# Ranks and slots one and two turns sooner, and one exponential for all shares, in the routing stage of a two-layer graph network

## The chip, the core and the metric

The kernel runs on one core of one Trainium2 chip. The metric is the device time of one execution in microseconds, the median of the runs. Five engines work side by side, each through its own row of instructions: TensorE (PE in the profile), VectorE (DVE), ScalarE (ACT), GpSimd (POOL) and SyncE (SP). They meet at semaphores.

## What is computed

Two layers, each a graph part, a mixer and a mixture of experts, on 3125 nodes with 256 numbers each. The change lies where layer 1 goes from the graph part to its experts. Cut to that, the reference reads:

```python
agg = segment_sum((xn @ weight)[src] * edge_weight[:, None], dst)      # second graph part
x = x + relu(agg) + mixer(xn)
tokens = layernorm(x)                                                   # no scale, no shift
probs = softmax(tokens @ router_w.T)
rw, re = top_k(probs, 2)                                                # two experts of eight
rw = rw / rw.sum(-1)
x = x + tokens + sum over e of combine[:, e] * (gelu(tokens @ w1[e] + b1[e]) @ w2[e] + b2[e])
```

The two shares of a token are the softmax of its two largest logits: with a = exp(second - first) they are 1 / (1 + a) and 1 minus that.

## The kernel before

The program is a row of stages; each ends with a barrier of all engines. The stage of interest is `second_graph`. The 3125 nodes are 25 tiles of 128 (`T`, g = 0 to 24). The sums over edges are already in `agg`. The stage multiplies them by the weight, adds them to `x`, normalizes, finds each token's logits and its two experts, gives each (token, expert) pair a row of the table `slots_d` in DRAM, expert after expert, and scatters the tokens there. The next stage, `second_experts`, reads that table in tiles of 128 rows, and multiplies each by its expert's weights.

Work goes through a software pipeline written out by hand: `pipeline(engine, [(lag, step), ...])` lets the engine run turn after turn, and in turn n each step takes tile n - lag, in the order of the list. Here it is all written out, with no loop left in the program (`first=NI, last=NI`). Turn by turn:

- TensorE: `turn_sums` (L2383, transposes), `project` (L2391, the weight), `turn_n` (L2400, transposes of normalized tokens), `score` (L2408, the logits), `rank_picks` (L2422, L2423).
- VectorE: `residual` (L2228, L2231, L2233: sum, statistics), `invert` (L2238, L2240), `place_picks` (L2284 to L2291) and `route` (L2254 to L2272).
- ScalarE: copies of TensorE's results (L2337, L2357, L2365), `spread_of` (L2344, a square root), `norm_x` (L2350), `exp_apart` (L2372, an exponential).
- GpSimd: two indirect DMAs a tile (L2211), 50 in all, each scatters 128 rows of 260 numbers.

The choice of experts works on groups of tiles, called parties: `PARTY = [3, 4, 4, 4, 4, 3, 3]`. For a party, `route` takes the logits in `pr`, finds the largest, its expert, and the second with its expert, and counts each expert's tokens tile by tile in `so_far`. `rank_picks` finds with two matmuls how many tokens ahead of this one chose the same expert. `place_picks` makes row numbers of these ranks (`slot`), and signals `slots_ready`, for which GpSimd waits. A step for parties does something only in the turn of the party's last tile. Before the change the lags are: `route` 6, `rank_picks` 8, `exp_apart` 8, `place_picks` 9. So for party 0, whose last tile is 2, VectorE chooses in turn 8, TensorE ranks in turn 10, and VectorE places in turn 11. `link(...)` makes VectorE wait for its own last instruction.

After the pipeline VectorE has a tail: the two shares from the exponentials (L2308 to L2310), then the number of tiles of each expert, and for each of 56 slot tiles its expert and its first row (`tile_expert`, `tile_at`, L2312 to L2329), which the next stage reads.

Of the kernel before, what the change touches and what calls it, by code (L numbers as in the profile page):

```python
# [6 lines left out]
ALU = mybir.AluOpType  # L7
ACT = mybir.ActivationFunctionType
# [12 lines left out]
R = 5  # L21
# [44 lines left out]
PARTY = [3, 4, 4, 4, 4, 3, 3]  # L66
PARTY_END = [sum(PARTY[:n + 1]) for n in range(len(PARTY))]
# [2086 lines left out]
def second_graph(nc, A, hold, bank, const, acc, agg, share, tile_expert, tile_at, bias1, bias2, slots_d, emptied, big_v, w, w_r, xrow):  # L2154
# [5 lines left out]
    with Stage(nc) as ctx:  # L2160
# [6 lines left out]
        most, place = S.sb("most", [P, 3, G]), S.sb("place", [P, 2, G])  # L2167
# [5 lines left out]
        r_step, apart, apart_exp, set_up = (S.sem(n) for n in ("r_step", "apart", "apart_exp", "set_up"))  # L2173
# [8 lines left out]
        whole = dict(turns=NI, width=R, first=NI, last=NI)  # L2182
# [8 lines left out]
        def ends_at(g):  # L2191
            return PARTY_END.index(g + 1) if g + 1 in PARTY_END else None
# [26 lines left out]
        def _(dve):  # L2219
            link = Steps(dve, r_step)  # L2220
# [22 lines left out]
            def route(i, j):  # L2243
                k = ends_at(i * R + j)
                if k is None:
                    return
                size = PARTY[k]
                order = const[:, C_ORDER:C_ORDER + E].unsqueeze(1).broadcast_to([P, size, E])
                dve.wait_ge(pr_ready, PARTY_END[k])
                if k > 0:  # L2250
                    dve.wait_ge(apart_exp, k)
                for n in range(2):
                    at = pr[:, k % 2, n, 0:size, :]
                    link(dve.tensor_reduce(most[:, n, 0:size], at, AX, ALU.max))  # L2254
                    link(dve.tensor_tensor(pick[:, n, 0:size], at, wide(most[:, n, 0:size], size), ALU.is_equal))

                    link(dve.tensor_tensor(rank[:, 0:size, :], pick[:, n, 0:size], order, ALU.mult))
                    link(dve.tensor_reduce(most[:, 2, 0:size], rank[:, 0:size, :], AX, ALU.max))
                    link(dve.tensor_tensor(pick[:, n, 0:size], rank[:, 0:size, :], wide(most[:, 2, 0:size], size), ALU.is_equal))
                    if n == 0:  # L2260
                        link(dve.tensor_scalar(xrow[:, PARTY_END[k] - size:PARTY_END[k], D + 1:D + 2],
                                               most[:, 2, 0:size].unsqueeze(2), -1.0, float(E), ALU.mult, ALU.add))
                        link(dve.scalar_tensor_tensor(out=pr[:, k % 2, 1, 0:size, :], in0=pick[:, 0, 0:size], scalar=-BIG, in1=at,
                                                      op0=ALU.mult, op1=ALU.add))
                dve.tensor_tensor(most[:, 2, 0:size], most[:, 1, 0:size], most[:, 0, 0:size], ALU.subtract).then_inc(apart, 1)
                if k > 0:
                    link(dve.tensor_copy(so_far[:, 0, :], so_far[:, PARTY[k - 1], :]))
                link(dve.tensor_tensor(taken[:, 0:size, :], pick[:, 0, 0:size], pick[:, 1, 0:size], ALU.add))
                if k == len(PARTY) - 1:
                    link(dve.tensor_tensor(taken[:, size - 1, :], taken[:, size - 1, :], used[:, :, 0], ALU.mult))  # L2270
                for t in range(size):
                    last = dve.tensor_tensor(so_far[:, t + 1, :], so_far[:, t, :], taken[:, t, :], ALU.add)  # L2272
                    if t < size - 1:
                        link(last)
                last.then_inc(picked, 1)
# [25 lines left out]
                                   ALU.is_ge, ALU.mult))  # L2301
            dve.tensor_copy(xrow[:, :, D:XW], token[:, :].unsqueeze(2).broadcast_to([P, T, XW - D])).then_inc(set_up, 1)
            dve.wait_ge(set_up, 1)
            pipeline(dve, [(1, residual), (2, invert), (9, place_picks), (6, route)], **whole)

            dve.wait_ge(apart_exp, len(PARTY))
            link(dve.tensor_scalar(share[:, 1, :], share[:, 1, :], 1.0, None, ALU.add))  # L2308
            link(dve.reciprocal(share[:, 0, :], share[:, 1, :]))
            link(dve.tensor_scalar(share[:, 1, :], share[:, 0, :], -1.0, 1.0, ALU.mult, ALU.add))  # L2310
            dve.wait_ge(ranked, len(PARTY))
            link(dve.tensor_scalar(tiles[:, :], n_of, 1.0 / P, None, ALU.mult))  # L2312
            link(dve.tensor_tensor(used[:, :, :], tiles[:, :].unsqueeze(2).broadcast_to([P, E, T]),
# [13 lines left out]
                                          in1=first_row[:, :], op0=ALU.mult, op1=ALU.add))  # L2327
            link(dve.tensor_copy(tile_at[:, 0, :], tile_expert[0:1, :]))
            link(dve.tensor_copy(tile_at[:, 1, :], first_row[0:1, :]))  # L2329

        @block.scalar
        def _(act):
# [31 lines left out]
                    once(act, slots_ready, k - 1)  # L2364
                act.activation(pr[:, k % 2, 0, t, :], l_ps, ACT.Copy).then_inc(pr_ready, 1)  # L2365

            def exp_apart(i, j):
                k = ends_at(i * R + j)
                if k is None:
                    return  # L2370
                act.wait_ge(apart, k + 1)
                act.activation(share[:, 1, PARTY_END[k] - PARTY[k]:PARTY_END[k]], most[:, 2, 0:PARTY[k]], ACT.Exp)\  # L2372
                   .then_inc(apart_exp, 1)

            pipeline(act, [(0, copy_sums), (2, spread_of), (3, norm_x), (4, copy_n), (5, copy_logits), (8, exp_apart)], **whole)

        @block.tensor
        def _(pe):
# [44 lines left out]
                pe.matmul(to, ones, so_far[:, 0:size, :].rearrange("p t e -> p (t e)"), start=False, stop=True)\  # L2423
                  .then_inc(ranked, 1)

            pipeline(pe, [(0, turn_sums), (1, project), (4, turn_n), (5, score), (8, rank_picks)], **whole)

def expert_weights(big_v):
# [263 lines left out]
```

## Time and profile before

| | |
|---|---|
| median of 3 runs | 2205.79 us (2203.96 to 2211.8) |
| the profiled execution, its own time | 2211.77 us |
| its span, first to last instruction | 2210.1 us |
| what lies around the span | 1.7 us |
| mean granted clock of TensorE | 0.814 |
| PE, DVE, ACT, POOL busy in the span | 72%, 57%, 40%, 48% |
| this stage in the span | some 1944 to 2051 us |

Times in the trace count from the span's start. A row of the timeline reads: start, duration, engine, line, operation, tiles written and read; in brackets the idle time of the engine before it, and what ended that.
### The profile page before, as it was taken

The page shows a single profiled execution, that of the slowest core. Times are in us where ns is not written, and L with a number is a line of the kernel's source. Part 1 is how long each engine was busy: PE and PEld are TensorE (multiplying, and loading weights), DVE is VectorE, ACT ScalarE, POOL GpSimd, SP SyncE. Part 2 cuts the span into 40 slices and gives each one's busy share as a digit, 9 for nine tenths or more (in the row PEclk, how much of TensorE's full clock was granted, in tenths as well). Part 3 has the DMA queues.
Part 4 walks back from the last instruction along what each step waited for, and adds up shares of the span by engine and source line. Part 5 has one row for each costly group of instructions (what it writes and reads, how often), then busy time and mean ns, then how long its engine had stood idle before and what let it go on. Part 6 is the DMA issues. An engine that isn't in the chain of part 4 may idle for free. (4 is left out here: it accounts for less than half of the span.)

```text
span 2210.1 us, 31483 instructions
## 1 busy us (share of the span) xinstructions
PE 1599.5 (72%) x7770; PEld 1248.9 (57%) x7770; DVE 1250.0 (57%) x3879; ACT 874.0 (40%) x2979; POOL 1068.4 (48%) x1173
## 2 busy tenths in 40 slices
PE   5535677666766676969999766776787776974792
PEld 4533444444444445959999654555565555763792
DVE  3523655556556587855777634554555554675435
ACT  2221655665656586645777421000011000153451
POOL 2751666666666500421222256666666666225341
PEclk8665677777777797989999777888888888995896
DMA  5741544444444302836555232333333333122786
GB/s 188 218 141 38 152 121 123 125 133 123 129 128 126 98 18 73 264 109 203 181 165 179 73 99 84 89 91 90 88 90 89 88 91 93 42 87 80 219 263 222
DMA packets 176882, 276.92 MB, mean 125 GB/s; under 512 B 28920, under 2 KB 132218, under 8 KB 176456
## 3 DMA queue, kind: packets, MB, share of 16 engines
q0 software_dynamic: 50352, 136.58, 21.5%
q1 hardware_dynamic: 82194, 94.23, 14.0%
q10 hardware_dynamic: 44166, 44.14, 6.0%
q8 instruction: 71, 1.16, 0.2%
q14 instruction: 99, 0.81, 0.1%
HBM read 202.35 MB, written 73.58 MB: 125 GB/s over the span
## 5 line engine op out<-in xcount | busy, mean ns | idle before, releaser
L501 POOL DMA_INDIRECT ring<-feat_d,src_lane x440 | 433.0, 984 | 282.9 <-issue 121.5
L1221 POOL DMA_INDIRECT rows<-xn_d,src_of x416 | 404.2, 972 | 236.3 <-issue 106.0
L1201 PE MATMUL bank<-ring,a_hot 128*128 128x260 f32 x880 | 319.0, 511 | 147.9 <-DVE ring L1100 64.7
L1392 PE MATMUL bank<-rows,big 128*128 x880 | 288.9, 445 | 138.8 <-DVE big L1300 66.7
L1130 ACT ACTIVATE ring<-ring 128x64 f32<-128x64 f32 x1540 | 376.7, 336 | 15.8 <-issue 14.8
L1201 PEld LDWEIGHTS bank<-ring,a_hot 128*128 128x128 f32 x880 | 204.8, 251 | 226.0 <-DVE ring L1100 83.6
L1309 DVE TENSOR_TENSOR big<-bank,big 128x256 f32 x440 | 186.6, 424 | 233.4 <-DMA m_bo<-in_L_mix_bo 112.1
L1392 PEld LDWEIGHTS bank<-rows,big 128*128 128x128 f32 x880 | 165.6, 211 | 236.7 <-issue 222.1
L1085 DVE TENSOR_TENSOR acc<-bank,acc 128x260 f32 x440 | 186.8, 425 | 145.9 <-PE bank L1201 59.4
L1362 ACT ACTIVATE big<-bank,a_col 128x256 f32<-128x256 f32 (+1 forms) x26 | 13.1, 553 | 417.4 <-issue 257.2
L1300 DVE TENSOR_SCALAR big<-const,dst_lane,ew_lane 128x128 f32<-128x128 f32 x440 | 151.8, 346 | 1.0 <-PEq L95 1.0
L184 POOL TENSOR_TENSOR e_norm_rstd<-e_norm_mv,const 128x1 f32<-128x1 f32 x75 | 42.7, 570 | 202.4 <-DVE e_norm_mv L180 202.4
L1992 PE MATMUL bank<-xn1T,top_w 128*128 128x128 f32 x800 | 99.6, 280 | 5.5 <-PEq L95 5.5
L1419 PE MATMUL bank<-big 128*128 128x256 f32 (+1 forms) x416 | 96.9, 376 | 5.4 <-ACT big L1372 5.4
L1372 ACT ACTIVATE big<-bank,a_b 128x256 f32<-128x256 f32 (+1 forms) x104 | 42.0, 464 | 145.4 <-PE bank L1419 123.2
L1992 PEld LDWEIGHTS bank<-xn1T,top_w 128*128 128x128 f32 x800 | 96.0, 197 | 5.8 <-issue 5.6
L2211 POOL DMA_INDIRECT slots_d<-xrow,g_slot x50 | 49.4, 987 | 95.9 <-DVE g_slot L2291 82.5
L2004 PE MATMUL bank<-top_w,e_mid 128*128 128x256 f32 x400 | 95.2, 383 | 0.0
L1431 PE MATMUL bank<-big 128*128 128x256 f32 x400 | 94.5, 379 | 0.0
L2499 POOL DMA_INDIRECT y_d<-e_y,e_to x56 | 55.2, 985 | 68.1 <-DVE e_to L2582 65.4
L1419 PEld LDWEIGHTS bank<-big 128*128 128x128 f32 x416 | 77.8, 193 | 18.0 <-issue 7.7
L1431 PEld LDWEIGHTS bank<-big 128*128 128x128 f32 x400 | 76.0, 190 | 10.3
(405 smaller groups left out, 2901.4 us busy)
## 6 DMA issues: line engine op xcount, KB each, us to landing
slots_d<-fold ACTq DMA_DIRECT2D x25, 1300.0 KB, 5.6
e_w_now<-in_L_ffn_w SPq DMA_DIRECT2D x56, 256.0 KB
a_dst_bc<-dst_lo_d SPq DMA_DIRECT2D x23, 512.0 KB
big<-in_L_ffn_W SPq DMA_DIRECT2D x16, 512.0 KB
e_x<-slots_d SPq DMA_DIRECT2D x56, 130.0 KB
ring<-feat_d,src_lane POOLq DMA_INDIRECT x440
rows<-xn_d,src_of POOLq DMA_INDIRECT x416
e_ys<-y_d SPq DMA_DIRECT2D x24, 256.0 KB
```

The costliest lines, as they stand in the source:

```text
L501: pool.indirect_dma_start(ring[:, q % RING, at, :], None, table, bass.IndirectOffsetOnAxis(ap=src_lane[:, n:n + 1], axis=0)).then_inc(gath ...
L1085: dve.tensor_tensor(to, bank[n % BANKS][:, 0:D + H], to, ALU.add).then_inc(added, 1)
L1130: last = act.activation(part[:, 0:DH], part[:, 0:DH], ACT.Copy, scale=part[:, DH:DW])
L1201: pe.matmul(bank[n % BANKS][:, 0:D + H], hot[:, q % HOTS, at, :], ring[:, q % RING, at, :], start=True, stop=True)\
L1221: pool.indirect_dma_start(rows[:, n % RING1, :], None, table, bass.IndirectOffsetOnAxis(ap=src_of[:, n:n + 1], axis=0)).then_inc(gathered[ ...
L1300: dve.tensor_scalar(hot[:, n % HOTS, :], const[:, C_IOTA:C_IOTA + P], dst_lane[:, n:n + 1], edge_weight[:, n:n + 1], ALU.is_equal, ALU.mul ...
L1309: dve.tensor_tensor(to, bank[n % 4][:, 0:D], to, ALU.add).then_inc(added, 1)
L1392: pe.matmul(bank[n % 4][:, 0:D], hot[:, n % HOTS, :], tile_of(rows, slots[n % 4]), start=True, stop=True)\
L1419: last = pe.matmul(mid_ps[q % 2][:, f * 2 * P:f * 2 * P + m * P], w1[:, k, n * P:(n + 1) * P], lnT[:, k, 0:m * P], start=(k == 0), stop=(k ...
L1431: last = pe.matmul(y_ps[:, t * D:(t + 1) * D], mid[:, f, t * P:(t + 1) * P], w2[:, f, :], start=(f == 0), stop=(f == FT - 1))
L1992: last = pe.matmul(mid_ps[half][:, f * P:(f + 1) * P], w1[:, half, k, f * P:(f + 1) * P], xn1T[:, k, bass.ds(g * P, P)], start=(k == 0), s ...
L2004: last = pe.matmul(y_ps[:, 0:D], mid[:, j, n * P:(n + 1) * P], w2[:, half, f, :], start=(n == 0), stop=(n == FT - 1))
```

## The change

Three things change in `second_graph`, and nothing elsewhere.

- `route` writes the difference of the two logits into `share[:, 0, ...]`, a row that is kept for all tiles, where it wrote into the scratch `most[:, 2, ...]`. It no longer waits for the exponential of the party before, but waits for its own subtraction. ScalarE's step `exp_apart`, seven exponentials in the pipeline, becomes one exponential of all 25 tiles behind the pipeline.
- `rank_picks` goes from lag 8 to lag 7 and stands behind `project`, ahead of `turn_n` and `score`; `place_picks` goes from lag 9 to lag 7.
- VectorE's turn begins with `place_picks` and `route`, and ends with `residual` and `invert`. The three instructions that finish the shares go from the head of VectorE's tail to its end.

```diff
@@ route, VectorE
                 dve.wait_ge(pr_ready, PARTY_END[k])
-                if k > 0:
-                    dve.wait_ge(apart_exp, k)
...
-                dve.tensor_tensor(most[:, 2, 0:size], most[:, 1, 0:size], most[:, 0, 0:size], ALU.subtract).then_inc(apart, 1)
+                dve.tensor_tensor(share[:, 0, PARTY_END[k] - size:PARTY_END[k]], most[:, 1, 0:size], most[:, 0, 0:size], ALU.subtract)\
+                   .then_inc(apart, 1)
+                dve.wait_ge(apart, k + 1)
@@ VectorE, pipeline and tail
-            pipeline(dve, [(1, residual), (2, invert), (9, place_picks), (6, route)], **whole)
-
-
-            dve.wait_ge(apart_exp, len(PARTY))
-            link(dve.tensor_scalar(share[:, 1, :], share[:, 1, :], 1.0, None, ALU.add))
-            link(dve.reciprocal(share[:, 0, :], share[:, 1, :]))
-            link(dve.tensor_scalar(share[:, 1, :], share[:, 0, :], -1.0, 1.0, ALU.mult, ALU.add))
+            pipeline(dve, [(7, place_picks), (6, route), (1, residual), (2, invert)], **whole)
+
+
             dve.wait_ge(ranked, len(PARTY))
...
             link(dve.tensor_copy(tile_at[:, 1, :], first_row[0:1, :]))
+            dve.wait_ge(apart_exp, 1)
+            link(dve.tensor_scalar(share[:, 1, :], share[:, 1, :], 1.0, None, ALU.add))
+            link(dve.reciprocal(share[:, 0, :], share[:, 1, :]))
+            link(dve.tensor_scalar(share[:, 1, :], share[:, 0, :], -1.0, 1.0, ALU.mult, ALU.add))
@@ ScalarE
-            def exp_apart(i, j):
-                k = ends_at(i * R + j)
-                if k is None:
-                    return
-                act.wait_ge(apart, k + 1)
-                act.activation(share[:, 1, PARTY_END[k] - PARTY[k]:PARTY_END[k]], most[:, 2, 0:PARTY[k]], ACT.Exp)\
-                   .then_inc(apart_exp, 1)
-
-            pipeline(act, [(0, copy_sums), (2, spread_of), (3, norm_x), (4, copy_n), (5, copy_logits), (8, exp_apart)], **whole)
+            pipeline(act, [(0, copy_sums), (2, spread_of), (3, norm_x), (4, copy_n), (5, copy_logits)], **whole)
+            act.wait_ge(apart, len(PARTY))
+            act.activation(share[:, 1, :], share[:, 0, :], ACT.Exp).then_inc(apart_exp, 1)
@@ TensorE
-            pipeline(pe, [(0, turn_sums), (1, project), (4, turn_n), (5, score), (8, rank_picks)], **whole)
+            pipeline(pe, [(0, turn_sums), (1, project), (7, rank_picks), (4, turn_n), (5, score)], **whole)
```

How the instructions move. VectorE's row, end of the choice of party 0 (one piece of the difference; a line with + is the changed kernel's, and its numbers from L2252 on are two less than before up to L2263):

```order
-L2272 TENSOR_TENSOR g_so_far<-g_so_far,g_taken 128x8 x3
+L2284 TENSOR_TENSOR g_rank<-bank,g_first_slot 128x24
+L2287 TENSOR_TENSOR g_pick<-g_pick,g_rank 128x24 x2
+L2288 TENSOR_REDUCE g_place<-g_pick 128x2x3
+L2291 CAST g_slot<-g_place 128x2x3
 L2228 SCALAR_TENSOR_TENSOR acc<-bank,acc 128x256
 L2231 BN_STATS g_stats<-acc 128x6
```

Before, the choice ends here, at the tail of turn 8; now the slots of party 0 are made here, at the head of turn 9, and its choice stands one residual and one inversion ahead.

TensorE's row, ranks of party 0, before:

```order
L2383 MATMUL bank<-const,big 128x128 x2
L2391 MATMUL bank<-big,g_sumsT 128x256 x2
L2400 MATMUL bank<-const,xrow 128x128 x2
L2408 MATMUL bank<-big,g_nT 128x8 x2
L2422 MATMUL bank<-g_taken,g_before_me 128x24
L2423 MATMUL bank<-g_so_far,const 128x24
```

and of the change (six lines less in their numbers):

```order
L2377 MATMUL bank<-const,big 128x128 x2
L2385 MATMUL bank<-big,g_sumsT 128x256 x2
L2416 MATMUL bank<-g_taken,g_before_me 128x24
L2417 MATMUL bank<-g_so_far,const 128x24
L2394 MATMUL bank<-const,xrow 128x128 x2
L2402 MATMUL bank<-big,g_nT 128x8 x2
```

The ranks stood at the end of turn 10; now they stand within turn 9, with the transposes and the logits of that turn behind them.

ScalarE's row behind party 0, before:

```order
L2365 ACTIVATE g_pr<-bank 128x8
L2372 ACT_TABLE_LOAD
L2372 ACTIVATE share<-g_most 128x3
L2337 ACTIVATE g_sumsT<-bank 128x256
L2344 ACT_TABLE_LOAD
L2344 ACTIVATE g_std<-g_mv,g_eps 128x1
```

and the end of its row in the changed kernel:

```order
L2357 ACTIVATE g_nT<-bank 128x256
L2365 ACTIVATE g_pr<-bank 128x8 x2
L2369 ACT_TABLE_LOAD
L2369 ACTIVATE share<-share 128x25
```

The exponential and the two loads around it are gone from the turns; one load and one exponential stand at the end.

## Rows read from the trace of the kernel before

**Rows 1.** chain that ended last: start us, us, what

```profile
2053.51 2.81 DMA e_x<-slots_d
```

**Rows 2.** GpSimd timeline (start us, us, instruction [idle before]); waits of L2211

```profile
1968.07 1.02 POOL L2211 DMA_INDIRECT slots_d<-xrow,g_slot  x1 [64.25 <-DVE g_slot L2291]
1969.39 1.00 POOL L2211 DMA_INDIRECT slots_d<-xrow,g_slot  x1 [0.30 <-issue]
...
1980.13 0.98 POOL L2211 DMA_INDIRECT slots_d<-xrow,g_slot  x1 [4.57 <-DVE g_slot L2291]
...
2033.86 0.98 POOL L2211 DMA_INDIRECT slots_d<-xrow,g_slot  x1 [4.17 <-DVE g_slot L2291]
...
2048.06 0.99 POOL L2211 DMA_INDIRECT slots_d<-xrow,g_slot  x1 [0.30 <-issue]
...
  DVE g_slot L2291: 82.5, 6
```

**Rows 3.** timeline of VectorE, the last slots and the end of its tail

```profile
2039.82 0.19 DVE L2291 CAST g_slot<-g_place 128x6 int32<-128x6 f32 x1
...
2046.08 0.40 DVE L2329 CAST tile_at<-g_first_row 1x56 int32<-1x56 f32 x1
```

**Rows 4.** timeline of VectorE and ScalarE, parties 0 and 1

```profile
1954.26 0.18 ACT L2365 ACTIVATE g_pr<-bank 128x8 f32<-128x8 f32 x1
...
1954.88 0.16 DVE L2240 SCALAR_TENSOR_TENSOR g_shift<-g_mv,g_rstd 128x1 f32<-128x1 f32 x1
...
1956.66 0.17 DVE L2254 TENSOR_REDUCE g_most<-g_pr 128x3 f32<-128x24 f32 x1
...
1960.01 0.42 DVE L2228 SCALAR_TENSOR_TENSOR acc<-bank,acc 128x256 f32<-128x256 f32 x1
...
1961.26 0.42 DVE L2228 SCALAR_TENSOR_TENSOR acc<-bank,acc 128x256 f32<-128x256 f32 x1
...
1966.07 0.18 DVE L2284 TENSOR_TENSOR g_rank<-bank,g_first_slot 128x24 f32<-128x24 f32 x1
...
1966.95 0.17 DVE L2291 CAST g_slot<-g_place 128x6 int32<-128x6 f32 x1
...
1968.30 0.18 DVE L2254 TENSOR_REDUCE g_most<-g_pr 128x4 f32<-128x32 f32 x1
...
1972.17 0.42 DVE L2228 SCALAR_TENSOR_TENSOR acc<-bank,acc 128x256 f32<-128x256 f32 x1
```

**Rows 5.** table loads (count | busy us, mean ns); VectorE behind them

```profile
L2344 ACT ACT_TABLE_LOAD x5 | 6.4, 1283 | 0.5 <-DVE g_mv L2233 0.5
L2372 ACT ACT_TABLE_LOAD x5 | 6.4, 1283 | 0.1
...
1965.80 0.16 DVE L2238 RECIPROCAL g_rstd<-g_std 128x1 f32<-128x1 f32 x1 [2.19 <-ACT g_std L2344]
```

**Rows 6.** a copy on VectorE beside a scatter; all scatters, ns min/median/max

```profile
1983.31 0.39 DVE L2267 COPY g_so_far<-g_so_far 128x8 f32<-128x8 f32 x1
...
L2211 POOL DMA_INDIRECT slots_d<-xrow,g_slot x50: 983/987/1022, 1968.1 to 2048.1; - x50
```

**Rows 7.** timeline of VectorE and TensorE, late results

```profile
1991.64 0.42 DVE L2228 SCALAR_TENSOR_TENSOR acc<-bank,acc 128x256 f32<-128x256 f32 x1 [4.41 <-DMA rows<-xn_d,src_of]
...
2024.03 0.60 PE L2423 MATMUL bank<-g_so_far,const 128*128 128x24 f32 x2
...
2032.00 0.18 DVE L2284 TENSOR_TENSOR g_rank<-bank,g_first_slot 128x24 f32<-128x24 f32 x1 [8.98 <-DMA rows<-xn_d,src_of]
```

**Rows 8.** stretches: PE, PEld, DVE, ACT, POOL, clock, DMA, GB/s; PE timeline

```profile
1956.60:1968.00 11.40, 8.58 (x54) 6.66 (x53) 8.18 (x41) 8.42 (x24) 0.00 (x0) 1.00 0.01 1
1980.00:1994.80 14.80, 11.73 (x54) 9.12 (x54) 9.24 (x45) 9.01 (x25) 7.89 (x9) 0.73 0.21 74
...
1994.45 1.91 PE L2391 MATMUL bank<-big,g_sumsT 128*128 128x256 f32 x4
...
1997.76 1.91 PE L2391 MATMUL bank<-big,g_sumsT 128*128 128x256 f32 x4
```

## The prediction

> **What bounds the kernel now.** The change touches one stage, the second graph stage, so I read the timeline to find where that stage ends and what it waits for, and not the busy shares of the whole span. The chain of waits says what comes next: the first expert stage is released by the load of a tile out of `slots_d` [rows 1], and that load can go only when the 50 scatters of the graph stage have landed. So the stage ends with the queue of scatters on GpSimd. In the timeline of GpSimd [rows 2] the reader sees that queue: the first scatter starts at 1968.07, the last at 2048.06. Two that follow each other start 1.291 us apart ((2048.06 - 2033.86) / 11). The 49 intervals would need 63.3 us; they took 80.0. The other 16.7 us are waits for slots: GpSimd waited six times for L2291 for 82.5 us, of which 64.25 are the first wait. The five others make 18.25 us, less the 0.30 that stands ahead of any scatter, five times, leaves 16.7. VectorE's own tail ends at 2046.48 [rows 3], sooner than the last scatter, so what moves the scatters moves the end, microsecond for microsecond, until VectorE's tail or the last slots come later than GpSimd gets free.
>
> **Step 1, the first slots.** A VectorE turn without a party is 1.25 us (residual at 1960.01, the next one at 1961.26), the choice for a party of three is 3.35 us (1956.66 to 1960.01), for four 3.87 us (1968.30 to 1972.17), and the placing of three 1.05 us (1966.07 to 1967.12) [rows 4]. Now the choice of party 0 stands at the head of turn 8. Its inputs are there (the third logits are copied at 1954.26 + 0.18), VectorE has ended turn 7 at 1955.04, so it runs from 1955.08 instead of 1956.66. I add 0.13 us for the new wait of VectorE for its own subtraction: no such wait stands there before; it costs nothing at the least, and at the most the 0.21 us that one of the choice's 16 small instructions takes on average, its wait included (3.35 / 16). I take the upper half, since the instruction behind it used to start at once. The choice ends at 1958.56, the rest of the turn (1.25) at 1959.81. Meanwhile TensorE, which has its two rank matmuls now behind the projection of turn 9 and before turning and scoring, needs some 0.8 us from 1958.6; they are done at 1959.4, so the wait at the head of turn 9 costs nothing: VectorE's rest of turn 8 hides them. If TensorE were late, it would cost the excess. Placing ends at 1960.9, GpSimd starts 0.95 us after that, as before (1967.12 to 1968.07). First scatter at 1961.84: 6.2 us sooner.
>
> **Step 2, the exponential.** Before, ScalarE loads a table for the exponential and another for the square root after it, five times each, 1.28 us a load, and VectorE sat idle 2.19 us for the root behind the pair of party 0 [rows 5]. Now 8 of the 10 loads of the stage are gone, one load and one exponential stand at the end of ScalarE's row, where VectorE's tail of some 6.5 us (from the last slots at 2039.99 to 2046.48) hides them. VectorE's period for a party of four becomes 4 x 1.25 + 3.87 + 0.13 + 1.1 = 10.1 us, where the first periods without anything odd were 12.1 (scatters of party 0 and 1: 1968.07 and 1980.13). The Trainium skill ("ScalarE: Activation LUTs", What ACT_TABLE_LOAD costs) prices a switch at 1283 ns and a drain of some 1380 more. This trace agrees with the first number (1283 ns) and shows no second part: the idle time is less than two loads; by the page a pair would be 5.3 us, and each party would gain 2.7 us more than I take.
>
> **Step 3, the waits that are left.** GpSimd needs 8 x 1.291 = 10.33 us for a party of four, more than the 10.1 in which VectorE makes its slots. Only after party 0, with six scatters (7.75 us), does it run dry: free at 1969.6, slots of party 1 at 1960.9 + 10.1 = 1971.0, start at 1971.95, a wait of 2.3 us. After that every batch finds its slots, and 43 intervals lead to a last start at 1971.95 + 55.5 = 2027.5. The two parties of three at the end are not paced by VectorE but by the row picks, ranks, turning, scoring, logits, choice; I work out some 7 us from one to the next, so the last slots come near 2016, and GpSimd is free for them only at 2021. Saving: 2048.06 - 2027.5 = **20.6 us**, which is 6.2 of step 1 and 16.7 - 2.3 = 14.4 of the waits.
>
> **A port.** VectorE's copy L2267 took 0.39 us while GpSimd scattered, and the scatters 983 to 1022 ns whatever stood beside them [rows 6]. With scatters throughout, that is at most 0.23 us in a period, 10.3 in all, still no more than GpSimd's 10.33. The Trainium skill ("SBUF — State Buffer", Who interferes with whom) speaks against sending more beside VectorE: the two share a port pair under an exclusive lock, and the loser blocks fully; a scatter could then be held for a whole instruction. The trace has no scatter that was held, so the sum takes nothing for it.
>
> **How much of 20.6 is steady.** Two periods of the trace were 14.7 and 14.6 us instead of 12.2, and the last wait came of a party whose rank matmuls have a modelled end of 2024.63 while VectorE, which waits for nothing else, went on at 2032.00, after 8.98 us idle. The idle 4.41 us before 1991.64 is likewise more than the tables explain [rows 7]. TensorE's results were late there by 2 to 7 us for no reason that I can read. Without these lags the old queue would have started its parties at 1968.1, 1980.1, 1992.3 and 2004.5 and its last scatter at 2004.5 + 27 x 1.291 = 2039.4, so the change would save 2039.4 - 2027.5 = 11.9 us. These are the ends: 11.9 and 20.6. The profiled execution took 2211.8 us, 6.0 over the median of 2205.8, and these lags are the one irregular thing in the stage; I take it that the median run has 6.0 us less of them. Sum against the profiled execution: 2211.8 - 20.6 = 2191.2; against the median: 2205.8 - 14.6 = 2191.2. **I predict 2191 us.**
>
> **Rivals.** *(a) TensorE paces the stage.* Its granted clock was 1.00 in the stretch of party 0 and 0.73 two parties later; it fell to the lower level (1.2 GHz) after pauses in which TensorE waited. At that level a turn is 3.31 us (1994.45 to 1997.76) [rows 8], and a party of four 4 x 3.31 + 1.25 for the ranks = 14.5 us. If the clock is low from party 2 on, slots come at 1971.0, 1985.5, 2000, 2014.5 and, with 19.5 us for the last two, 2034; the last scatter starts at 2034 + 0.95 + 6.45 = 2041.4, a saving of 6.7: 2199 us. For it: the stage dropped twice and then stayed low. Against it: the pauses that preceded a drop are the table and lag pauses, and the first go away.
> *(b) Late results remain.* If the lags strike again as in the profile, two periods grow to some 12.2 and the tail by 7: last start some 2036, a saving against such a run of 12, near 2194 to 2197 in a mean run.
> *(c) Slower: lockstep.* VectorE now waits at the head of its turn, for ranks and for logits, with the residual and the inversion queued behind it; TensorE waits for the picks with turning and scoring behind. If TensorE runs at 1.2 GHz, the head wait is no longer hidden, each side stands while the other works, and the choice (3.9 us) is added to the 14.5: 18.4 us a party. Slots at 1971.0, 1989.4, 2007.8, 2026.2, last ones near 2049, last scatter at 2056.4: 8.3 us later, 2214 us. It decides from a period of about 16.5 us, since (2040.0 - 1971.0 - 19.5) / 3 is 16.5. Against it: in party 0 the order leaves 0.4 us of slack at the higher level, and TensorE has two turns of work that need nothing of VectorE's current turn.
> That the change does not do what it says I exclude: the printed order has the ranks and placings where the text says.
>
> **How the numbers follow.** A measurement of this kernel can tell about 0.5%, 11 us, from no change. The forecast (a saving of 10 to 21) has a chance of 0.68, (a) 0.15, (b) 0.12, (c) 0.05. The range reaches from 2184.5 (the full 20.6 against the median, with 0.7 for the shorter waits of a luckier run) to 2200 (rival a). Faster by over 0.5%, below 2194.8: 0.60 of the 0.68, and 0.12 from the better ends of (a) and (b), 0.72. Within: 0.25. Slower by over 0.5%: 0.03, since (c) at its own price stays under 11 us.
>
> **What would show it.** Right: first scatter near 1961.8, one wait of some 2.3 us after the sixth scatter and none over 1 us later, last scatter near 2027; two table loads in the stage; VectorE's periods near 10.1. Step 1 is wrong if VectorE is idle before L2252 or L2284 of party 0. Step 2 is wrong if it is idle before L2238. Step 3 is wrong if GpSimd still waits over 2 us between later parties; then TensorE's clock in the stretch tells (a) from (b). The whole is wrong if the first tile load of the next stage does not follow the last scatter by the 5.4 us that lie between 2048.06 and 2053.51 now [rows 1, 2].

## The result, and the profile after

| | before | changed |
|---|---|---|
| median | 2204.18 us (2187.98 to 2217.38, 20 runs) | 2192.87 us (2179.36 to 2202.3, 20 runs) |
| ratio | | 0.9954, interval 0.9935 to 0.9974 |
| span of the profiled execution | 2210.1 us | 2177.7 us |

The changed kernel is 11.3 us faster at the median; 2191.0 was forecast. The two profiled spans differ by 32.4 us, and that is not the change: the stage of interest begins (`g_eps`, L2293, VectorE's first instruction in it) at 1941.52 us before and at 1918.42 after, so 23.1 us lie in code that the change doesn't touch; the profiled execution after was the fastest of its 20. I therefore count every time of the stage from that instruction.

| counted from L2293 | before | changed | forecast |
|---|---|---|---|
| first scatter starts | 26.55 | 19.70 | 6.2 sooner |
| last scatter starts | 106.54 | 95.13 | 20.6 sooner |
| next stage's first load is issued | 110.83 | 101.87 | as the last scatter |

GpSimd's timeline in the changed kernel, the start of each batch of scatters, the last scatter of the second batch, and the last of all (columns as in [rows 2]):

```profile
1938.12 1.02 POOL L2211 DMA_INDIRECT slots_d<-xrow,g_slot  x1 [56.74 <-DVE g_slot L2291]
...
1948.69 0.98 POOL L2211 DMA_INDIRECT slots_d<-xrow,g_slot  x1 [3.08 <-DVE g_slot L2291]
...
1957.73 0.99 POOL L2211 DMA_INDIRECT slots_d<-xrow,g_slot  x1 [0.31 <-issue]
1962.12 0.98 POOL L2211 DMA_INDIRECT slots_d<-xrow,g_slot  x1 [3.40 <-DVE g_slot L2291]
...
1975.58 0.99 POOL L2211 DMA_INDIRECT slots_d<-xrow,g_slot  x1 [3.43 <-DVE g_slot L2291]
...
1989.02 0.98 POOL L2211 DMA_INDIRECT slots_d<-xrow,g_slot  x1 [3.42 <-DVE g_slot L2291]
...
2013.55 0.99 POOL L2211 DMA_INDIRECT slots_d<-xrow,g_slot  x1 [0.30 <-issue]
```

Batches start 13.4 us apart, not 10.1. Less the 0.30 that stands ahead of any scatter, the four waits are 12.1 us; before they were 16.7 [rows 2], and 2.3 were forecast. They are no accident: they are alike to 0.35 us, and a second profile of the kernel (below) repeats them.

Where the time goes, in the timeline of all engines beside the second batch (idle of the engine in brackets):

```profile
1951.64 0.42 DVE L2228 SCALAR_TENSOR_TENSOR acc<-bank,acc 128x256 f32<-128x256 f32 x1 [1.24 <-PE bank L2385]
...
1953.14 0.38 PE L2394 MATMUL bank<-const,xrow 128*128 128x128 f32 x2
...
1955.83 0.38 ACT L2357 ACTIVATE g_nT<-bank 128x256 f32<-128x256 f32 x1 [2.15 <-DMA rows<-xn_d,src_of]
...
1957.45 0.42 PE L2417 MATMUL bank<-g_so_far,const 128*128 128x32 f32 x2
...
1960.22 0.19 DVE L2284 TENSOR_TENSOR g_rank<-bank,g_first_slot 128x32 f32<-128x32 f32 x1 [1.81 <-DMA rows<-xn_d,src_of]
```

ScalarE copies at 1955.83 what L2394 began at 1953.14, and VectorE goes on at 1960.22 with ranks whose modelled end is 1957.87. Both waits begin in the batch that begins at 1948.69 and ends at 1958.72. A matmul's end is modelled, so the row alone doesn't say whether TensorE, its signal or the waiting engine was late. The trace has more: the time of each semaphore update that it recorded. The update of L2394 (modelled end 1953.52) is at 1955.81, that of L2402 (1953.87) at 1959.32, that of L2417 (1957.88) at 1960.19, and each time the waiting engine starts 0.02 us behind the update. So the waiting engine is prompt and the update is late, by up to 5.9 us in this stage. VectorE's tail shows it with no TensorE and no modelled end in it, each instruction waiting for VectorE's own last one:

```profile
2006.24 0.16 DVE L2314 TENSOR_TENSOR g_edge<-g_edge,g_tiles 128x1 f32<-128x1 f32 x1
2006.74 0.16 DVE L2314 TENSOR_TENSOR g_edge<-g_edge,g_tiles 128x1 f32<-128x1 f32 x1 [0.34 <-DVE g_edge L2314]
2008.14 0.16 DVE L2314 TENSOR_TENSOR g_edge<-g_edge,g_tiles 128x1 f32<-128x1 f32 x1 [1.24 <-DVE g_edge L2314]
...
2012.34 0.57 DVE L2316 TENSOR_TENSOR g_past<-const,g_edge 128x392 f32<-128x392 f32 x1 [1.18 <-DVE g_edge L2315]
...
2018.05 0.18 DVE L2329 TENSOR_SCALAR share<-share 128x25 f32<-128x25 f32 x1
```

The six L2314 and L2315 have their updates 0.32 to 1.22 us after their ends. The tail takes 13.1 us (last slots ready at 2005.15, shares at 2018.23; 12.9 to the start of its last instruction) instead of the 6.5 of [rows 3]. It ends 3.7 us after the last scatter has ended, and so the stage now ends with VectorE, not GpSimd: from the last scatter's start to the next stage's first load it is 6.74 us (2013.55 to 2020.29) where it was 4.29. In e0, e3 and e4 below, whose tails are slow too, the load likewise goes 2.1 us behind VectorE's last instruction.

```profile
2020.29 0.36 SPq L2472 DMA_DIRECT2D e_x<-slots_d  x1
```

The tables went as forecast, one of each in place of five (groups of ScalarE in the stage, as [rows 5]):

```profile
L2344 ACT ACT_TABLE_LOAD x1 | 1.3, 1283 | 0.5 <-DVE g_mv L2233 0.5
L2369 ACT ACT_TABLE_LOAD x1 | 1.3, 1283 | 0.0
```

And the clock, by batch (columns as in [rows 8]): the upper level up to 1947.4, the lower to 1950.8, then half of each period at the lower (1957.67 to 1964.5 and 1971.32 to 1978.15), and the lower throughout from 1985 on.

```profile
1938.00:1948.70 10.70, 8.04 (x46) 6.14 (x45) 9.04 (x44) 5.69 (x20) 5.98 (x7) 0.94 0.21 76
1948.70:1962.10 13.40, 9.89 (x52) 8.51 (x51) 9.20 (x44) 6.27 (x20) 7.88 (x8) 0.75 0.23 81
```

### The profile page after: what moved, and what is told of

Its sections match the earlier page's. It is cut to its first block and busy times, and to the rows that moved or that the text cites. A ratio compares the mean times of both kernels' runs of the same rounds, so it can differ in the third digit from the quotient of the medians.

```text
span 2177.7 us, 31463 instructions
## 1 busy us (share of the span) xinstructions
PE 1591.3 (73%) x7770; PEld 1251.9 (57%) x7770; DVE 1251.5 (57%) x3879; ACT 862.1 (40%) x2965; POOL 1067.5 (49%) x1173
## 2 busy tenths in 40 slices
DMA packets 176882, 276.92 MB, mean 127 GB/s; under 512 B 28920, under 2 KB 132218, under 8 KB 176456
## 5 line engine op out<-in xcount | busy, mean ns | idle before, releaser
L1362 ACT ACTIVATE big<-bank,a_col 128x256 f32<-128x256 f32 (+1 forms) x26 | 13.1, 552 | 416.9 <-PE bank L1407 177.5
L2004 PE MATMUL bank<-top_w,e_mid 128*128 128x256 f32 x400 | 95.7, 384 | 0.0
L2211 POOL DMA_INDIRECT slots_d<-xrow,g_slot x50 | 49.4, 987 | 83.8 <-DVE g_slot L2291 70.1
L1419 PEld LDWEIGHTS bank<-big 128*128 128x128 f32 x416 | 77.6, 192 | 11.9 <-issue 1.5
```

The source lines that it names most:

```text
L1419: last = pe.matmul(mid_ps[q % 2][:, f * 2 * P:f * 2 * P + m * P], w1[:, k, n * P:(n + 1) * P], lnT[:, k, 0:m * P], start=(k == 0), stop=(k ...
L2004: last = pe.matmul(y_ps[:, 0:D], mid[:, j, n * P:(n + 1) * P], w2[:, half, f, :], start=(n == 0), stop=(n == FT - 1))
```

## The experiments

My theory after the result: **held signals**. While scatters run for some time, semaphore updates of TensorE, and in the tail of VectorE itself, are posted late, and many come out soon after the batch ends. It isn't every signal: in the same batch TensorE starts L2416 0.05 us after VectorE's last L2272 ends, VectorE's linked instructions of the choice follow each other without idle time, and none of ScalarE's recorded updates in the stage is over 0.01 us late. With it the period is a loop: 8 scatters (10.0 us), 1.5 until VectorE resumes, 1.1 of placing, 0.8 to the first scatter of the next batch, 13.4. The rivals: **clock** (TensorE at 1.2 GHz paces), **order** (an engine's row has the wrong thing ahead), and **chance**.

**e0_changed_again.** The changed kernel itself, for repeatability.

> The changed kernel once more, to see what in the stage repeats. Stage time is counted from VectorE's first instruction of the stage (L2293) to the start of the last scatter: 106.5 us before the change, 95.1 us in the first profile of the change. If the waits of GpSimd between parties (3.1 to 3.4 us each, four of them) are a fixed part of the pattern, they come again within 0.5 us each and the stage takes 93 to 97 us. If TensorE's late results are chance, one or two of the four waits are under 1 us and the stage takes 86 to 92 us.

2195.46 us against 2204.16, ratio 0.9955 (0.9927 to 0.9984). The stage repeats to 0.5 us: first scatter 19.99, last 95.37, next load 102.39, slots 13.4, 13.5, 13.4 us apart. The waits are a pattern, not chance.

**e1_scatters_held.** No scatter before all slots are ready.

```diff
@@ GpSimd
+            pool.wait_ge(slots_ready, len(PARTY))
             for g in range(T):
                 send(g)
```

> The changed kernel, but GpSimd waits for the slots of the last party before its first scatter, so that no scatter runs beside the choice. Theory A (scatters beside the choice make TensorE's signals late): the periods of VectorE from party to party fall from 13.4 us to 10.1 to 10.8, VectorE is idle less than 0.3 us ahead of L2284, and the last slots come some 68 to 73 us after the stage's start where they came near 86. Theory B (lateness comes of TensorE's lower clock or its pauses): periods stay at 12.5 to 13.5 and the last slots near 84 to 87. The run as a whole is slower by 45 to 60 us under both, since 50 scatters follow at the end.

One run, 2234.39 us; what counts is VectorE without scatters beside it. Slots come 10.0, 11.2, 12.8, 11.1 us apart for the parties of four, the longest idle at the ranks is 1.6, and the tail takes 6.4 us. Of the 551 updates of TensorE, VectorE and ScalarE in this stretch none is over 0.02 us late. So the scatters make the late signals and all of the long tail, but not the whole of the 13.4: neither expectation had periods of 11 to 13 us with no wait at the ranks, nor the last slots at 80.7 us of the stage (68 to 73 and 84 to 87 were expected). What is left goes with the clock, which fell here too, first at 27.8 us of the stage (29.0 in the change): the period of 10.0 has 1.0 us of the lower level, those of 11.1 and 11.2 have 4.3, and the 12.8 has 6.0; its waits are for the projection.

```profile
1965.00:1978.00 13.00, 10.99 (x56) 9.40 (x55) 9.20 (x46) 6.78 (x21) 0.00 (x0) 0.76 0.00 1
```

**e2_before_one_exp** and **e3_order_only.** The two halves of the change apart. e2 is the kernel before with the one exponential (and the shares last in the tail); e3 is the changed kernel with seven exponentials again (the definition of `exp_apart` and the count that VectorE's tail waits for, both as before the change, are left out here):

```diff
@@ e3, ScalarE
-            pipeline(act, [(0, copy_sums), (2, spread_of), (3, norm_x), (4, copy_n), (5, copy_logits)], **whole)
-            act.wait_ge(apart, len(PARTY))
-            act.activation(share[:, 1, :], share[:, 0, :], ACT.Exp).then_inc(apart_exp, 1)
+            pipeline(act, [(0, copy_sums), (2, spread_of), (3, norm_x), (4, copy_n), (5, copy_logits), (8, exp_apart)], **whole)
```

> The kernel before with only the first part of the change: one exponential behind the pipeline, the difference kept in share, lags and order as before. If the table loads were on the path by the 2.2 us that VectorE sat idle behind them, four or five times, the stage falls from 106.5 to 97 to 101 us, and the whole by 5 to 10 us. If lateness of TensorE fills what the loads leave (as in the changed kernel, whose periods are 13.4 us without loads), the stage falls by under 4 us. The first scatter comes 2.5 us sooner than before under both (26.6 us after the stage's start to 24).

> The changed kernel with the exponentials back in ScalarE's turns (lag 8, seven of them), so only the lags and the order differ from before. By the forecast's split this is worth the 6.2 us of the first scatter: first scatter 19.7 to 20.5 us after the stage's start, stage 100 to 101 us. If the loads cost nothing because TensorE is late anyway, the stage is 95 to 97 us, like the full change. If loads cost 2.2 us a party: 102 to 104 us.

e2: 2195.45, ratio 0.9958 (0.9935 to 0.998), last scatter at 101.92, 4.6 sooner than before. e3: 2197.61, ratio 0.9971 (0.9944 to 0.9998), last scatter at 99.45, 7.1 sooner. Their sum, 11.7, is the 11.4 of both together. In e3 the first slots are as early as in the change (first scatter 20.24): early ranks bring the first scatter forward, the exponential shortens periods. e2 lies between its two expected ranges (5.5 to 9.5 us sooner, or under 4), e3 half a microsecond under its own. In both, GpSimd still waits: 2.83, 4.61, 3.87, 4.21 in e2 and 5.28, 3.76, 4.09, 4.09 in e3.

**e4_tail_of_turn.** The changed kernel with slots and choice at VectorE's tail.

```diff
-            pipeline(dve, [(7, place_picks), (6, route), (1, residual), (2, invert)], **whole)
+            pipeline(dve, [(1, residual), (2, invert), (7, place_picks), (6, route)], **whole)
```

> The changed kernel with slots and choice back at the tail of VectorE's turn (residual and inversion first), lags and single exponential as changed. What the place in the turn is worth: the choice of party 0 comes one turn body and a wait for TensorE later, 1.6 us, so the first scatter 21.3 to 21.8 us after the stage's start instead of 19.7 to 20.0. If the later periods are a loop between GpSimd's batches and TensorE's late signals (13.4 us), they stay 13.4 and the last scatter starts near 97. If VectorE paced them, they would stay 10 to 11 and the place would cost the same 1.6.

One run, 2197.4 against 2202.28. The last scatter starts at 109.21, 14 us later than in the change and later than before; batches start 16 to 17 us apart:

```profile
1974.70 0.98 POOL L2211 DMA_INDIRECT slots_d<-xrow,g_slot  x1 [6.88 <-DVE g_slot L2291]
...
1990.87 0.98 POOL L2211 DMA_INDIRECT slots_d<-xrow,g_slot  x1 [6.14 <-DVE g_slot L2291]
```

VectorE stood 21.0 us in 13 waits at its residual for the projection. Both expectations for the last scatter (near 97, or the same 1.6 us later) were missed by over 10 us. The place at the head of the turn thus makes the two shorter lags pay here; the whole time of a single run, which is even below the median before, says nothing on it.

**e5_five_parties** and **e7_parties_and_shares.** `PARTY = [3, 5, 6, 6, 5]`; e7 also takes the three share instructions into the next stage.

> The changed kernel with PARTY = [3, 5, 6, 6, 5] instead of [3, 4, 4, 4, 4, 3, 3]. Theory C (TensorE's signals of the ranks get out only some 1.3 us after GpSimd's batch has drained, so each batch is followed by 3.1 to 3.4 us of waiting for its successor): the waits stay 3.1 to 3.5 us each but there are three or so instead of four, last scatter 92 to 94 us after the stage's start. Theory D (a fixed lateness of 1.5 to 2 us in a period that VectorE paces): a batch of 6 tiles takes GpSimd 15.5 us and VectorE 6 x 1.25 + 4.9 + 1.3 + 2 = 15.7, so the waits shrink under 1.3 us, last scatter 86 to 90.

> e5 with the three instructions that finish the shares moved from VectorE's tail in this stage to the start of VectorE's row in the next, where it is idle until the first tile is loaded. In the changed kernel the tail ends 99.6 us after the stage's start and the last scatter has started at 95.1, so the tail is what ends the stage. Expected: the first tile load of the next stage is issued 1.5 to 2.5 us sooner relative to e5, the whole 1 to 3 us faster than e5, and 3 to 8 us faster than the changed kernel.

Slower: 2208.96, ratio 1.0032 (1.0003 to 1.006), and 2206.94, 1.002 (0.9996 to 1.0043); last scatters at 109.3 and 110.7. No expectation had this. With batches of 10 and 12 scatters VectorE stood longer, each time until a batch had run out. Timelines of GpSimd and VectorE in e5, the end of one batch:

```profile
1976.52 0.98 POOL L2211 DMA_INDIRECT slots_d<-xrow,g_slot  x1 [0.30 <-issue]
1977.80 0.98 POOL L2211 DMA_INDIRECT slots_d<-xrow,g_slot  x1 [0.30 <-issue]
...
1980.42 0.42 DVE L2228 SCALAR_TENSOR_TENSOR acc<-bank,acc 128x256 f32<-128x256 f32 x1 [5.76 <-DMA rows<-xn_d,src_of]
```

The last scatter ends at 1978.78, VectorE goes on 1.64 us later. Longer batches hold more: the theory in kind, though I had its size wrong. The tails of e5 and e7 are prompt (5.7 us to the last `tile_at`) though scatters had run for 11.3 us when they began, so moving the shares in e7 could gain nothing: its next load goes 4.4 us behind its last scatter, e5's 4.2. The slow tails (the change, e0, e3, e4) began when scatters had run for 15.6 to 16.5 us, and their first late update comes at 17.1 to 17.6; in e5 and e7 the last `tile_at` was written by 17.0.

**e6_pause_in_batch.** GpSimd waits, ahead of a batch's last tile, for the next party's ranks.

```diff
-                pool.wait_ge(slots_ready, party_of(g)[0] + 1)
+                party, t = party_of(g)
+                pool.wait_ge(slots_ready, party + 1)
+                if 0 < party < len(PARTY) - 1 and t == PARTY[party] - 1:
+                    pool.wait_ge(ranked, party + 2)
```

> The changed kernel, but GpSimd keeps the last two scatters of a party (1 to 5) back until the ranks of the next party are signalled, so that its queue is empty when TensorE ranks. Theory C (signals get out on draining): the six scatters end 7.4 us after the batch began, the ranks are signalled within 1 us of their modelled end, VectorE waits less than 0.6 us at L2284, and the next batch finds its slots ready; period 12.4 to 13.0 us instead of 13.4, the wait now inside the batch. Theory D (any overlap of scatters and choice costs a fixed lateness): VectorE still idle 1.3 to 1.8 us at L2284, period 14 us or more.

One run, 2194.82 against 2202.28. The idle of VectorE at the ranks of the large parties is gone, as the theory wants, but slots still come 11.2 to 13.5 us apart (12.4 to 13.0 expected), since other waits (L2228) took its place: a miss in that half. What did change is the tail: from the last slots at 2021.77 to the shares it takes 6.5 us, and the first load goes 4.25 us after the last scatter's start, at 100.58 us of the stage, 1.3 sooner than in the change. The kernel before had its prompt tail beside scatters too [rows 2, 3], and so has e2, whose first load goes 4.25 us after its last scatter: in these three, as in e5 and e7, the queue had stood still 0.4 to 11.3 us before the tail; in the change it had run since 1989.02, 16.1 us.

**e8_shares_next_stage, e9_short_batches, e10_one_pause, e11_one_pause_again.** e8 is the changed kernel with the shares finished in the next stage; its pipeline is the change's, instruction for instruction. e9 sends the first expert's row of every tile, then the second's (batches of four). e10 is e6 with one pause only:

```diff
@@ e9
-            for g in range(T):
-                send(g)
+            for k0 in range(2):
+                for g in range(T):
+                    send(g, k0)
@@ e10
-                if 0 < party < len(PARTY) - 1 and t == PARTY[party] - 1:
+                if party == len(PARTY) - 2 and t == PARTY[party] - 1:
                     pool.wait_ge(ranked, party + 2)
```

> The changed kernel with only the three share instructions moved from the end of VectorE's tail to the start of its row in the next stage. Loop and lateness untouched: periods 13.4 us, last scatter 95 us after the stage's start. If the tail is what ends the stage, the first tile load of the next stage is issued 100 to 101 us after the stage's start instead of 101.9 and 102.4; if the landing of the last scatter ends it, 101.9 or more. The whole 1 to 2 us faster than the change, less than a measurement tells.

> The changed kernel with the scatters of the first choices as they come and those of the second choices behind all of them, so a batch beside the choice is 4 scatters (5.2 us) long, not 8. Theory C' (TensorE's signals begin to be late 4.5 to 8 us after a batch began and are freed 1.0 to 1.7 us after it ended): hardly any is late, VectorE waits under 0.3 us at L2284 for parties 1 to 4, period 10 to 11.5 us as with no scatters at all (10.0 to 12.8), last slots 78 to 82 us after the start. Theory E (any scatter beside the choice delays the signals, in proportion to their number): periods 11.5 to 12.5. The stage as a whole is longer (25 scatters, 32 us, follow the last slots).

> The changed kernel with one pause: GpSimd keeps the last two scatters of party 5 back until the ranks of party 6 are signalled, so that VectorE's tail begins beside a young batch. With e6's five pauses the tail took 6.3 us from the last slots (12.9 us in the changed kernel) and the next stage's first load came 100.6 us after the stage's start. Expected here: periods 13.4 as changed, the tail 6 to 9 us, last scatter at 95.5 to 97, first load at 99.5 to 101. If the slow tail has nothing to do with the length of the run of scatters, the tail stays 11 to 13 us and the load at 102 or later.

> The kernel of e10_one_pause once more, since its first run fell where the kernel before takes 1902.8 us and where no signal came late (placings 10.1 us apart, one wait of 2.48 us, last scatter at 86.7 us of the stage), and all runs of the changed kernel itself fell where the kernel before takes 2202 to 2204 us. Theory H (the late signals hang on the device the kernel runs on, not on the edit of e10): if this run falls where the kernel before takes some 2203 us, the placings are 13.4 us apart again, GpSimd waits four times for 3.1 to 3.4 us, the last scatter starts at 95 to 96.5 us of the stage, and only the tail of VectorE is short (under 7 us instead of 12.9), so that the next stage's first load goes 4.3 us behind the last scatter and not 6.7: near 100 us, 1 to 2 us sooner than in the changed kernel, ratio 0.993 to 0.996. Theory E (it is the one wait in the last large batch that keeps the signals prompt): placings 10.1 us apart and last scatter at 87 us there as well, 8 us sooner than in the changed kernel, ratio 0.990 to 0.992. If it falls where the kernel before takes some 1903 us, both expect the figures of e10 again, and nothing is told apart.

These four ran where the kernel before itself takes 1900 to 1903 us instead of 2202 to 2206: on other chips, 11 and 7, where e0 to e7 ran on 13 and 4. I call the first kind A (all runs above) and this one B. All runs on B were also made later than those on A, so a chip and whatever else changed in between are not told apart. Results: e8 1894.71, ratio 0.9957 (0.9941 to 0.9973); e9 1915.69 in one run against 1902.8; e10 1890.8, ratio 0.9935 (0.9916 to 0.9953); e11, e10's kernel again, 1891.13, ratio 0.9948 (0.9934 to 0.9962).

The surprise is in e8's stage. GpSimd's timeline, all waits over 1 us and the last scatter:

```profile
1656.02 1.02 POOL L2211 DMA_INDIRECT slots_d<-xrow,g_slot  x1 [46.95 <-DVE g_slot L2291]
...
1665.98 0.98 POOL L2211 DMA_INDIRECT slots_d<-xrow,g_slot  x1 [2.48 <-DVE g_slot L2291]
...
1721.80 0.99 POOL L2211 DMA_INDIRECT slots_d<-xrow,g_slot  x1 [0.30 <-issue]
```

VectorE's timeline, ranks and slots of two parties, and its tail:

```profile
1664.09 0.18 DVE L2284 TENSOR_TENSOR g_rank<-bank,g_first_slot 128x32 f32<-128x32 f32 x1
...
1665.01 0.17 DVE L2291 CAST g_slot<-g_place 128x8 int32<-128x8 f32 x1
...
1675.24 0.17 DVE L2291 CAST g_slot<-g_place 128x8 int32<-128x8 f32 x1
...
1713.58 1.13 DVE L2314 TENSOR_TENSOR g_edge<-g_edge,g_tiles 128x1 f32<-128x1 f32 x6
```

and its stretches:

```profile
1665.00:1675.00 10.00, 7.71 (x53) 6.33 (x52) 8.86 (x44) 5.53 (x20) 6.89 (x7) 1.00 0.23 82
1675.00:1685.00 10.00, 7.93 (x54) 6.53 (x53) 8.83 (x45) 5.75 (x21) 7.86 (x8) 1.00 0.30 108
```

This is the forecast's stage. Slots come 10.1, 10.2, 10.0, 10.1 us apart, with scatters beside without a break; there is one wait of 2.48; VectorE has no idle at the ranks of a party of four; the six linked L2314 run in 1.13 us where on A they took 4.2; and the last scatter starts 65.8 us after the first (65.7 was forecast, 1961.84 to 2027.5; 75.4 on A). e10 and e11 show the same to 0.1 us (one wait of 2.48, 65.9 and 65.8, tail 6.5). The clock stays at 1.00 until 1692.7, 57.5 us into the stage. And no update that can be put to its instruction, in the whole trace of any of the four runs on B (some 6,900 each), is over 0.04 us late, where the changed kernel on A has 334 of 5,313 over 0.15 us late. So held signals are not a property of this program alone: the same row of instructions has them on A (the after profile, e0, and the variants, on chips 13 and 4 at least) and not on B (e8 and e10 on one chip, e11 on another). e9's question, whether batches of four escape the hold, could not be answered on B, where there is none, and the figures expected of e8 and e10 (periods of 13.4, last scatter near 95) were those of A; the second rows of all tiles, 25 scatters, stood behind the last slots, and the last scatter started at 112.4 us. e11 was meant to see e10 on A and fell on B too, so whether e10 has its gain on A is open; e6, its nearest kin there, gave one run only.

The difference between A and B is not this stage's alone. On A the 334 late updates lie in stretches with indirect DMAs, but for two within 10 us behind one; the rest of the 497 us without them (755 to 1252) has none. The page's groups of GpSimd, in the changed kernel on A:

```profile
L501 POOL DMA_INDIRECT ring<-feat_d,src_lane x440 | 430.1, 977 | 281.8 <-issue 120.8
L1221 POOL DMA_INDIRECT rows<-xn_d,src_of x416 | 405.6, 975 | 228.7 <-issue 108.6
```

and in e10 on B:

```profile
L501 POOL DMA_INDIRECT ring<-feat_d,src_lane x440 | 430.5, 978 | 149.5 <-issue 128.4
L1221 POOL DMA_INDIRECT rows<-xn_d,src_of x416 | 404.2, 972 | 141.7 <-issue 114.3
```

An indirect DMA costs the same on both. GpSimd's waits between them are 132.3 and 87.0 us longer on A, 219 of the 289 us by which the spans of these two kernels differ. It is the stages with indirect DMAs that are longer there. Dense work is not: L2004's 400 matmuls take 384 ns on A and 382 on B.

## Why the prediction was right, and where it was not

- **Step 1, the first slots: right.** 6.85 us sooner, 6.2 forecast; VectorE is not idle at L2252 or L2284 of party 0.
- **Step 2, tables: right** in number (two loads, 1283 ns each) and in kind: alone (e2) it brings the last scatter 4.6 us forward. No second part of a switch's cost was seen.
- **Step 3, "after that every batch finds its slots": wrong on A, right on B.** Waits fell by 4.6 us and not by 14.4, since the period for four is 13.4 and not 10.1: the step took signals at no time and the clock at its upper level. On B the step holds to 0.2 us. The 7 us "from one to the next" of the parties of three, for which the prediction shows no rows, measured 8.4 to 8.6 on both; GpSimd was busy anyway.
- **"They are the one irregular thing in the stage": wrong.** The late results are regular on A. That is the mechanism of rival (b), but not its chance: they did not strike again, they were always there. The number survived since I had taken 6.0 off the saving against the median (14.6); the stage gave 9.0 at the next load (8.4 in e0), which lies in the interval of the ratio (5.7 to 14.3 us) though the median's difference is 11.3. So that 2191 came out near is in part luck: 20.6 was over twice what came, the deduction of 6.0 had a wrong reason, and the median before, of 20 runs, lies 1.6 us under that of the three I had.
- **The step "VectorE's tail of some 6.5 us hides them", and the load following the last scatter as before: wrong on A.** The tail takes 12.9 us while scatters run, ends last, and gives back 2.5 us (6.74 against 4.29). On B it takes 6.5 and is hidden. The 5.4 us of the forecast ran to the landing's start; counted to the load's issue the figure of before is 4.29.
- **Rival (a), clock: not at its price of 14.5 us a period,** but not nothing. The lower level was granted for 6.8 us in a period of 13.4; without scatters (e1) one period of four reached 12.8 at 0.76, and on B none passed 10.2 with the clock at 1.00. How much of the 3.3 us is the clock's and how much the hold's, one run bears on: the same three periods take 11.7 us on average in e1, without a late signal, and 10.1 on B. My estimate from these: half of the 3.3 us would be there without the hold. Why the clock falls some 29 us earlier in the stage on A, e1 included, is not known.
- **Rival (c), lockstep: did not come.** TensorE does stand 2.0 to 2.2 us ahead of the ranks' first matmul, and the turn goes on. It is e4, the other order of VectorE's turn, that with 16.9 us came near the 18.4 of (c).
- **The port:** no scatter was held in the changed kernel: their mean is 987 ns, the median of [rows 6]. In e8 it is 993, and one reads 1.36 us. The Trainium skill's warning ("SBUF — State Buffer", Who interferes with whom) is the nearest thing to what A shows, but not the same: there an access is blocked, here instructions keep their durations and signals are late, those of TensorE above all.

**Estimate for B.** The kernel before has no profile there. Its stage without lags was worked out in the prediction as 11.9 us longer than the change's; e10 and e11 measured 12.4 (0.0065 x 1902.8) and 9.9 us (0.0052 x 1900.1), the change's pipeline with one wait that ended nothing. That agrees, but is not a test of the changed kernel itself on B, which wasn't run.

**What stays open.** Why signals are held on A, and from when in a batch: the start varies. Neither the number of DMA packets (176,882) nor those of the instruction queues (71 and 99) differs between the changed kernel on A and e8 on B; what of the two chips does, no run here shows. One rival is untested: the recording itself. The traces on A hold 18,400 to 18,800 semaphore updates, those on B 33,700, and of the 551 in this stage's choice the change's trace has 402 while e1 and e8 have all. So where signals are late, records are missing too. Every run listed has a span and a granted clock, so none is known to have run unrecorded, and a part of the recording in the lateness can't be excluded. The version I would keep on B is e10, faster than the kernel before in both its runs (0.9935, 0.9948); on A it has not been run, and that it would beat the change there is only suggested, by e6's shorter end. On B it starts its last scatter 2.6 us later than 49 intervals would need.

## What to carry to other kernels

Idle times that a profile names after a transfer of another stage, or that no instruction explains, are not noise until a second profile says so: had I compared the two long periods of [rows 4, 7] with the batches of scatters beside them, the loop would have been there to read. The semaphore updates in the trace of the kernel before say it outright: that of the ranks L2423, with a modelled end of 2024.63, is recorded at 2031.98, and VectorE goes on at 2032.00. A schedule worked out from durations should name what it takes for signals: here they cost under 0.04 us on B and up to 5.9 us in this stage on A. When a queue is the bound, ask also what ends second: VectorE's tail was 4 us from taking over, and it did.

## What was not expected of the hardware

- On A, semaphore updates of TensorE were posted up to 5.9 us late in this stage of the changed kernel once indirect DMAs had run for 3 to 5 us, while ScalarE's were prompt, and VectorE's were 0.3 to 1.2 us late in the tail. The last ones of a batch came 1.2 to 1.6 us after it ended (after: batches end at 1945.62 and 1958.72, L2284 starts at 1946.79 and 1960.22; e5: 1978.78 and 1980.42), others in its midst (1955.81), and in the tail there is still 0.5 us of lateness at 2017.25, 2.7 us after the last scatter. On B, with the same instructions, nothing was late.
- The same program takes 2204 us on A and 1902 on B, and three quarters of the difference stand as GpSimd's idle time between the indirect DMAs of two stages.
- Two placements of a step that need the same work (e4 and the change) gave periods of 16.2 to 16.9 and 13.4 us on A.
